# A hybrid conv, state-space and FFN kernel: layer norm variance on all channel partitions, and the conv loop written out

## The reference

```python
x = x + _L0_conv_ref(_gn(x), ...)                 # x is [8, 32, 16, 16]
t = _to_tokens(x)
t = t + _L1_attn_ref(_ln_t(t), ...)               # a selective state-space scan
t = t + _L1_ffn_ref(_ln_t(t), ...)                # a few attention/FFN steps chosen by the data
x = _from_tokens(t, x)

def _ln_t(v, eps=1e-05):
    m = jnp.mean(v, axis=-1, keepdims=True)
    s = jnp.var(v, axis=-1, keepdims=True)
    return (v - m) / jnp.sqrt(s + eps)

# in _L0_conv_ref: nine taps, each sampled bilinearly at learned positions
sampled = bilinear_sample(x, ys, xs)
out = jnp.einsum('bkhwc,ock->bohw', sampled, w)
```

## Time and profile before

| | |
|---|---|
| median of 3 runs | 377.03 us (374.76 to 381.24) |
| the profiled execution | 376.58 us, of which 374.8 us are the span of its instructions |
| PE busy in the span | 268.1 us (72%) |
| DVE busy | 299.2 us (80%) |
| ACT busy | 162.6 us (43%) |
| POOL busy | 238.8 us (64%) |
| mean granted PE clock | 0.750 of full speed |

### The profile page before, as it was taken

The page is one execution under the profiler, slowest core; times in us unless marked ns, Lnnn a source line. Parts: engine busy times, 40 slices in busy tenths (PEclk is TensorE's granted clock), DMA queues, the critical chain, the costliest instruction groups (busy, mean ns, idle before and its releaser), DMA issues. The chain is left out here.

```text
span 374.8 us, 4192 instructions
## 1 busy us (share of the span) xinstructions
PE 268.1 (72%) x1390; PEld 101.5 (27%) x1396; DVE 299.2 (80%) x232; ACT 162.6 (43%) x259; POOL 238.8 (64%) x116
## 2 busy tenths in 40 slices
PE   5987999997862765576547755775567688789883
PEld 1436776664420000000000000000000143236521
DVE  1089999972688999999999999999999974324732
ACT  1064776662535543444434452554354341224420
POOL 1245899980029999999999999999999730000000
PEclk9898999999986555555565556556555599998998
DMA  6000000000020000000000000000000000000000
GB/s 219 33 0 2 2 0 0 0 0 1 23 62 2 0 1 0 0 0 2 0 0 0 0 1 0 2 1 0 0 0 0 1 2 1 12 16 0 0 0 28
DMA packets 2495, 3.83 MB, mean 10 GB/s; under 512 B 687, under 2 KB 1712, under 8 KB 2480
## 3 DMA queue, kind: packets, MB, share of 16 engines
q1 hardware_dynamic: 2348, 3.58, 3.3%
q10 hardware_dynamic: 132, 0.07, 0.1%
HBM read 2.59 MB, written 0.26 MB: 8 GB/s over the span
## 5 line engine op out<-in xcount | busy, mean ns | idle before, releaser
L362 POOL TENSOR_TENSOR pool<-pool 128x1024 f32<-128x1024 f32 x62 | 144.6, 2352 | 37.7 <-DVE pool L645 37.7
L645 DVE TENSOR_TENSOR_SCAN pool<-ps,pool 128x1024 f32<-128x1024 f32 x63 | 143.8, 2283 | 2.0 <-ACT ps L468 2.0
L957 PE MATMUL ps<-pool,picks 96*128 96x512 bf16 x120 | 59.5, 597 | 72.5 <-DVE pool L645 72.5
L466 ACT ACTIVATE ps<-ps,ssmw 128x1020 f32<-128x1020 f32 x64 | 69.4, 1084 | 74.7 <-DVE pool L634 74.7
L963 PE MATMUL ps<-pool,chosen 128*32 128x512 f32 x256 | 60.0, 1033 | 0.7 <-DVE pool L662 0.7
L634 DVE TENSOR_TENSOR pool<-pool,ps 128x1024 f32<-128x1024 f32 x49 | 58.5, 1195 | 1.2 <-PE ps L938 1.2
L957 PEld LDWEIGHTS ps<-pool,picks 96*128 96x128 bf16 x120 | 7.8, 109 | 146.5 <-DVE pool L645 146.5
L418 ACT ACTIVATE pool<-ps 128x1024 f32<-128x1024 f32 x36 | 34.7, 1024 | 20.4 <-PE ps L860 20.4
L860 PE MATMUL ps<-cst,pool 128*128 128x128 f32 x288 | 36.4, 282 | 3.7 <-DVE pool L224 3.7
L356 POOL TENSOR_TENSOR pool<-pool 128x1024 f32<-128x1024 f32 x15 | 35.2, 2346 | 1.5 <-ACT pool L454 1.5
L860 PEld LDWEIGHTS ps<-cst,pool 128*128 128x128 f32 x288 | 32.8, 144 | 10.3 <-issue 10.3
(11 more groups left out here) (128 smaller groups left out, 207.5 us busy)
## 6 DMA issues: line engine op xcount, KB each, us to landing
ssmw<-ssm_w_dram SPq DMA_DIRECT2D x1, 896.0 KB, 8.5
pool<-pool SPq DMA_DIRECT2D x12, 64.0 KB, 2.0
offw<-offset_w_dram SPq DMA_DIRECT2D x1, 576.0 KB, 6.3
cst<-const_dram SPq DMA_DIRECT2D x1, 426.0 KB, 6.8
xq<-x_dram SPq DMA_DIRECT2D x2, 128.0 KB
out_dram<-fin SPq DMA_DIRECT2D x2, 128.0 KB
convw<-conv_w_dram SPq DMA_DIRECT2D x1, 144.0 KB, 6.8
pool<-w_up_dram SPq DMA_DIRECT2D x2, 64.5 KB
```

The costliest lines, as they stand in the source:

```text
L362: pool_e.tensor_tensor(to, of, cn, ALU.mult).then_inc(prod_ready, 1)
L466: act.activation(decay[:, :, 1:HW], decay[:, :, 1:HW], ACT.Exp, scale=wt["a"][:, PER * g + j:PER * g + j + 1]).then_inc(da_ready, 1)
L645: dve.tensor_tensor_scan(state[e % GROUPS], slot(e), dbx[e % GROUPS], 0.0, ALU.mult, ALU.add)\
L957: ins = pe.matmul(slot(e)[:, column_half(c)], picks[:, j * 128:(j + 1) * 128], stack[0:96, g * SEQ + c * BANK:g * SEQ + (c + 1) * BANK], s ...
```

## The change

The conv loop is written out in Python on all four engines, so every index is a constant; PE reads the weights directly from `zs`, and the tile `zk`, its 18 copies on POOL and their semaphore are gone. The turn of the next chunk now also stands ahead of the tap sum at what was the end of a row, and the hats beyond the last chunk are not made. The layer norm sums the squares with one matmul whose weights are `mean` (1/32 in each 32x32 block, made once on POOL), so that the variance stands on all 128 channel partitions and 512 columns; root and reciprocal are taken on that 128x512 tile. The transposes, the widening copy and the second `keep_warm(4)` are gone.

```diff
+        root = sb("root", [128, TOK])
+        mean = sb("mean", [128, 128])
...
-            eng.wait_ge(samp_turned, 6 * it + 2 * j + 2)
+            if it:
+
+                eng.wait_ge(samp_turned, 6 * (it - 1) + 2 * j + 2)
...
+            pool_e.tensor_tensor(mean[:, :], ident, part["centre"], ALU.subtract).then_inc(mean_ready, 1)
...
-            with pool_e.Fori(0, ROWS) as kk:
-                for half in range(HALVES):
-                    it = HALVES * kk + half
-                    sampling_chunk(pool_e, it, 2)
-                    pool_e.wait_ge(z_ready, 8)
-                    for j in range(3):
-                        k = 3 * kk + j
-
-                        pool_e.wait_ge(chunk_summed, 3 * it + j + 1)
-                        pool_e.tensor_copy(zk[j], zs[:, half, :, :, bass.ds(k * C, C)]).then_inc(zk_ready, 1)
-
+            for it in range(HALVES * ROWS):
+                sampling_chunk(pool_e, it, 2)
...
-                act.activation(root[:, :], bank(2)[:, 0:16], ACT.Sqrt, bias=eps[:, :]).then_inc(ln_sd, 1)
+                act.activation(root[:, :], bank(2), ACT.Sqrt, bias=eps[:, :]).then_inc(ln_sd, 1)
...
-            with dve.Fori(0, ROWS) as kk:
-                for half in range(HALVES):
-                    for j in range(2):
-                        sampling_chunk(dve, HALVES * kk + half, j)
-
-                    distances(half, kk + 1)
+            for it in range(HALVES * ROWS):
+                for j in range(2):
+                    sampling_chunk(dve, it, j)
+                if it + HALVES < HALVES * ROWS:
+                    distances(it + HALVES)
...
-                step(dve.reciprocal(inv[:, :], root[:, :]))
+                step(dve.reciprocal(root[:, :], root[:, :]))
                 settle()
-                dve.tensor_copy(inv_wide[:, :].rearrange("p (k c) -> p k c", k=16),
-                                inv[:, :].unsqueeze(2).broadcast_to([128, 16, C])).then_inc(ln_inv, 1)
-                dve.wait_ge(ln_turned, n + 1)
-                return dve.tensor_tensor(dst[:, :], cen[:, :], bank(2), ALU.mult)
+                return dve.tensor_tensor(dst[:, :], cen[:, :], root[:, :], ALU.mult)
...
-            def tap_sum(it, half, j):
-                pe.wait_ge(zk_ready, 3 * it + j + 1)
-                pe.wait_ge(turned_ready, 6 * it + 2 * j + 2 + 3)
+            def tap_sum(it, j):
+                kk, half = divmod(it, HALVES)
+                k = 3 * kk + j
+                pe.wait_ge(turned_ready, 6 * it + 2 * j + 2)
                 for hh in range(2):
                     for q in range(PAIRS):
-                        ins = pe.matmul(bank(0)[quad(q), half * HW:(half + 1) * HW], zk[j][:, q, hh, :],
+                        ins = pe.matmul(bank(0)[quad(q), half * HW:(half + 1) * HW],
+                                        zs[:, half, q, hh, k * C:(k + 1) * C],
                                         sampT[j][:, q, hh, :], start=False, stop=False)
...
-                for c in range(4):
-                    ins = pe.matmul(bank(2)[:, PAIRS * c:PAIRS * (c + 1)], sq[:, c * 128:(c + 1) * 128], part["pairs"],
-                                    start=True, stop=True)
-                ins.then_inc(ln_var, 1)
-                keep_warm(4)
-                pe.wait_ge(ln_inv, n + 1)
-                for c in range(4):
-                    ins = pe.transpose(bank(2)[:, c * 128:(c + 1) * 128], inv_wide[:, c * 128:(c + 1) * 128], ident)
-                ins.then_inc(ln_turned, 1)
+                pe.wait_ge(mean_ready, 1)
+
+                pe.matmul(bank(2), mean[:, :], sq[:, :], start=True, stop=True).then_inc(ln_var, 1)
```

More of the change, by code:

```diff
@@ L76, in hybrid_kernel @@
         sq = sb("sq", [128, TOK])
-        root = sb("root", [128, 16])
-        inv = sb("inv", [128, 16])
-        inv_wide = sb("inv_wide", [128, TOK])
+        root = sb("root", [128, TOK])
+        mean = sb("mean", [128, 128])
         tn = sb("tn", [128, TOK])
@@ L110, in hybrid_kernel @@
         sampT = [region("conv", 8 * HW).rearrange("p (q h n) -> p q h n", q=PAIRS, h=2) for _ in range(3)]
-        zk = [region("conv", 8 * C).rearrange("p (q h o) -> p q h o", q=PAIRS, h=2) for _ in range(3)]
         xs = region("ssm", SEQ)
@@ L181, in hybrid_kernel @@
         samp_made = [sem(f"samp_made{j}") for j in range(3)]
-        samp_turned, turned_ready, zk_ready, chunk_summed, conv_done = map(
-            sem, ["samp_turned", "turned_ready", "zk_ready", "chunk_summed", "conv_done"])
+        samp_turned, turned_ready, chunk_summed, conv_done = map(
+            sem, ["samp_turned", "turned_ready", "chunk_summed", "conv_done"])
         ln_in, ln_cen, ln_sq, ln_var, ln_sd, ln_out = map(
             sem, ["ln_in", "ln_cen", "ln_sq", "ln_var", "ln_sd", "ln_out"])
-        ln_inv, ln_turned = sem("ln_inv"), sem("ln_turned")
+        mean_ready = sem("mean_ready")
         delta_done, xs_done, b_done, gate_in_done, c_done = map(
@@ L220, in sampling_chunk @@
             eng.wait_ge(hat_ready, it + 1)
-            eng.wait_ge(samp_turned, 6 * it + 2 * j + 2)
-            now = hat[:, bass.ds(it, 1), :, 2 * j:2 * j + 2, :].rearrange("p i c o y -> p (i c) o y")
+            if it:
+                eng.wait_ge(samp_turned, 6 * (it - 1) + 2 * j + 2)
+            now = hat[:, it, :, 2 * j:2 * j + 2, :]
             eng.tensor_tensor(samp[j].rearrange("p c (y x) -> p c y x", y=SIDE),
@@ L310, in _ @@
             pool_e.memset(wbd[:, :, :], 0.0).then_inc(wbd_zeroed, 1)
-            pool_e.sem_inc(chunk_summed, 3)
             pool_e.wait_ge(spread_in, 16)
@@ L384, in _ @@
             act.activation(gsd[:, :], mv[:, :, 1], ACT.Sqrt, bias=eps[:, :]).then_inc(gn_sd, 1)
-            act.sem_inc(turned_ready, 3)
             def evacuate_filters(n):
@@ L398, in hats @@
                 act.wait_ge(hat_abs, i + 1)
-                v = hat[:, bass.ds(i, 1), :, :, :].rearrange("p i c o y -> p (i c o y)")
+                v = hat[:, i, :, :, :].rearrange("p c o y -> p (c o y)")
                 act.activation(v, v, ACT.Relu, bias=1.0, scale=-1.0).then_inc(hat_ready, 1)
@@ L407, in _ @@
             evacuate_filters(3)
-            with act.Fori(0, ROWS) as kk:
-                for half in range(HALVES):
[L411 to L422, removed]
+            for it in range(HALVES * ROWS):
+                for j in range(3):
+                    if it:
+                        act.wait_ge(chunk_summed, 3 * (it - 1) + j + 1)
+                    for side in range(2):
+                        s = 2 * j + side
+                        act.wait_ge(samp_turned, 6 * it + s + 1)
+                        act.activation(sampT[j][:, 2 * side:2 * side + 2].rearrange("p q h n -> p (q h n)"),
+                                       bank(2 + 2 * (s % 3), 2), ACT.Copy).then_inc(turned_ready, 1)
+                    if j == 1 and it + HALVES < HALVES * ROWS:
+                        hats(it + HALVES)
             def layer_norm(n):
@@ L558, in _, with distances @@
                .then_inc(off_ready, 1)
[L560 to L563, removed]
+            def distances(i):
+                kk, half = divmod(i, HALVES)
+                pos = bank(1)[:, half * HW:(half + 1) * HW].rearrange("p (c o) -> p c o", c=8)[:, :, 6 * kk:6 * kk + 6]
+                v = hat[:, i, :, :, :]
                 dve.tensor_tensor(v, pos.unsqueeze(3).broadcast_to([128, 8, 6, SIDE]),
@@ L572, in _ @@
             for half in range(HALVES):
-                distances(half, 0)
-            with dve.Fori(0, ROWS) as kk:
-                for half in range(HALVES):
-                    for j in range(2):
-                        sampling_chunk(dve, HALVES * kk + half, j)
-                    distances(half, kk + 1)
+                distances(half)
+            for it in range(HALVES * ROWS):
+                for j in range(2):
+                    sampling_chunk(dve, it, j)
+                if it + HALVES < HALVES * ROWS:
+                    distances(it + HALVES)
             dve.wait_ge(conv_done, 1)
@@ L824, in keep_warm @@
                     pe.matmul(bank(at), zero_bf[:, 0:128], zero_bf[:, :], start=True, stop=True)
-            pe.sem_inc(samp_turned, 6)
             pe.wait_ge(zero_set, 1)
@@ L853, in turn @@
                     s = 2 * j + side
-                    pe.wait_ge(turned_ready, 6 * it + s + 1)
+                    if 6 * it + s >= 3:
+                        pe.wait_ge(turned_ready, 6 * it + s - 2)
                     for q in range(2):
@@ L862, in turn @@
                     ins.then_inc(samp_turned, 1)
-            def tap_sum(it, half, j):
-                pe.wait_ge(zk_ready, 3 * it + j + 1)
-                pe.wait_ge(turned_ready, 6 * it + 2 * j + 2 + 3)
+            def tap_sum(it, j):
+                kk, half = divmod(it, HALVES)
+                k = 3 * kk + j
+                pe.wait_ge(turned_ready, 6 * it + 2 * j + 2)
                 for hh in range(2):
                     for q in range(PAIRS):
```

(9 more changed lines are left out.)

## The result

| | before | after | ratio, 95% interval |
|---|---|---|---|
| first comparison | 375.89 us (4 runs) | 385.95 us (382.51 to 388.74, 4 runs) | 1.024 [1.015, 1.033] |
| second (e7_again below) | 378.72 us (17 runs) | 384.41 us (383.54 to 388.66, 6 runs) | 1.018 [1.011, 1.025] |

By these ratios the changed kernel is slower by about 2%, 7 to 9 us, where +4 us was forecast; the medians lie 10.1 and 5.7 us apart. The ratios leave out runs more than 1.5% above the fastest of the same kernel, the medians don't, and the profiled execution (388.74 us, span 386.9 us) is such a run; where that matters, a second profile of the same kernel stands beside it (e7_again, span 381.8 us). The first median lies 0.95 us above the top of the stated range (385 us), the second within it.

The account below looks back on a forecast made before the run. PE was taken to set the conv loop's pace, held up by copies, and the norms to be pure chains. -2.9 + 2.3 + 1.7 + 2.3 + 0.65 = +4.05 on 376.6 gave 380.65, or 381.0 us in the runs' terms; range 376.5 to 385.

Parts of the forecast that it names:

- The conv loop, -2.9 us: Conv loop: without POOL's copies PE runs 2.90 us a tap to the last, ending 2.9 us sooner.
- the rival of the ports: Conv loop: DVE and POOL contend, PE waits for products, 2.3 us lost, sum 383.3 us; chance 0.12.
- The layer norms, +2.3 us each: Both layer norms: the 128x512 reciprocal at 3.33 us makes each norm 2.3 us longer.
- The line through 128x2 and 128x16: Layer norms: reciprocal's 165 and 252 ns, 6.2 ns an element, extended to 512 elements as 3.33 us.
- PE's clock behind the first norm, +1.7 us: First projections: after PE's 4.9 us pause the clock is 0.50 for 3.4 us, costing L911 1.7 us.
- The rival that the clock stays down: First projections: both groups double, 7.4 us in place of 1.7, sum 386.7 us; chance 0.11.
- PE's clock behind the second norm, +0.65 us: Ahead of L1011: the same pause loses 1.7 us, of which 0.65 shows.
- the 1.06 us to spare: Behind the second norm: PE's slack before L1097, which waits for a weight DMA, taken as 1.06 us.

Follow-up runs that it names:

- e7_again: The changed kernel run once more, unchanged: 384.41 us (6 runs).
- e5_copies: Conv loop written out, layer norms of before, but POOL's 18 weight copies and PE's waits for them put back: 377.89 us, ratio 1.007 to the kernel before.
- e1_conv: The changed kernel with the layer norms of before, so only the conv loop is written out: 373.89 us, ratio 0.995 to the kernel before.
- e3_warm: The changed kernel with 21 matmuls on zeros filling PE's pause in both layer norms: 384.11 us, ratio 1.018 to the kernel before.
- e2_norm: The kernel before with only the new layer norms put in, conv loop of before: 383.27 us, ratio 1.014 to the kernel before.
- e10_bridge: The changed kernel with 3 matmuls on zeros between projections L889 and L882, the norms' pause left: 380.29 us, ratio 1.013 to the kernel before.
- e8_warm_again: The kernel of e3_warm run again, unchanged: 383.37 us (7 runs), ratio 1.013 to the kernel before.
- e9_fill8: The changed kernel with 8 matmuls on zeros, not 21, in PE's pause in each norm: 385.87 us, ratio 1.028 to the kernel before.
- e4_rsqrt: The changed kernel with ACT's Abs_reciprocal_sqrt in place of root and reciprocal, its table brought in ahead: 372.01 us, ratio 0.986 to the kernel before.

## Why the prediction fell short

By its own steps, against the profiles of the changed kernel:

- **The conv loop, -2.9 us.** Measured -2.7 (57.1 to 54.4 us), every tap 2.90 us as forecast; e5_copies shows that the copies carry it, e1_conv that it stands alone. Right in mechanism and size. The hand-written order of DVE and POOL held: the rival of the ports didn't come.
- **The layer norms, +2.3 us each.** Measured +2.4 each. The line through 128x2 and 128x16 gave 3.33 us for the reciprocal; it takes 3.35 in both norms, though the base was fourteen elements. The missing 0.1 us is the root, 0.69 us where the square's 0.60 was taken. The Trainium skill's repeat count of 8 (VectorE: DVE Perf Modes, section on the fixed hardware budget), read as 8 cycles an element, gave an estimate of 4.3 us. The measurement decides: from 252 ns at 16 elements to 3353 ns at 512 it is 6.25 ns an element, six cycles at its 0.96 GHz.
- **PE's clock behind the first norm, +1.7 us.** The clock fell as forecast, but the size of this term was wrong, and it is the step that was off: "the granted clock is 0.50 for 3.4 us" was carried over from the two restarts of the earlier trace rows. Here it was 0.50 for 10.2 us, 9 of them after the restart. L889 lost the 1.7 us, and L882 another 2.1 in full, 3.8 together. e3_warm takes all of it back by filling the pause, and e2_norm shows it without the conv change. The rival that the clock stays down was right in its mechanism, and at 7.4 us for the two groups its price was twice the measured 3.8. The length of a fall wasn't the constant that it was taken for: ahead of the loop, where nothing was changed, the first restart of the earlier trace rows has 3.4 us at 0.50 in the profile of before and 6.8 in both of the changed kernel. Whether the 1.11 us pause behind L889 lengthened it is open; e10_bridge speaks for it, in one profile whose other fall was shorter too.
- **PE's clock behind the second norm, +0.65 us.** Measured +0.46 (11.84 to 12.30 us), and right in its mechanism: the slower matmuls on zeros used up the 1.06 us to spare and 0.45 more. Other profiles with the same pause have 0 to 1.0 us.
- **Not in the sum.** The steps above make -2.7 + 2.4 + 3.8 + 2.4 + 0.5 = +6.4 us, 1.7%, which is within both measured intervals. By its ratio the first comparison shows 9.0 us; the further 2.6 us fit the attention stage, which in the first profile of the changed kernel lost 4.4 us to a fall of the clock against the profile of before, in e7_again gained 0.5, and differs as much between e3_warm and e8_warm_again, which are one kernel. In the spans, 6.4 + 4.4 + 1.5 (the start) = 12.3 us of the 12.1 between the profiles of before and after. The start of the kernel varies too (30.6, 32.1 and 31.5 us to the first turn, the clock at 0.50 for 3.6 or 6.8 us of it). Which fall the attention stage gets goes with the moment at which it begins. In all three profiles with 10.2 us (the changed kernel, e3_warm, e9_fill8) it begins 10.5 to 10.7 us into the stage, in all five with 3.4 us (before, e1_conv, e4_rsqrt, e5_copies, e10_bridge) 5.8 to 6.0 us into it, and four have none. What sets that moment, and why some kernels meet the long fall more often (most of the executions of e3_warm and e8_warm_again, by their times, fewer of before's), is open.

## What to carry to other kernels

Before an operation is moved onto a wider tile, price it by the element from two sizes of the same operation in the trace: here a line through 2 and 16 elements gave the time of 512 to 1%, and an operation that costs six cycles an element is not a small step any more. A pause that a longer step opens on PE is to be priced by what PE does next, as a range: the falls behind such pauses lasted 3.4, 6.8 or 10.2 us here, and the length of one wasn't that of another. Filling the whole pause took the loss back, filling 1.9 of its 5.0 us did not; filling the next short pause too may help, but isn't shown. Copies on POOL beside DVE work with two SBUF inputs cost what they wait for, not what they move: the last one, with DVE idle, took 0.40 us, the median one 2.45.

## What the runs showed of the hardware beyond the expected

- After the pause of 5 us the clock came back only within L882, 9 us after PE had restarted, in four profiles (the changed kernel, e7_again, e2_norm, and e9_fill8 with 3.25 us of pause); in e10_bridge it was back 4.9 us after. The first restart of the earlier trace rows had 3.4 us at 0.50 in five profiles and 6.8 in seven, with the same code there.
- In the attention stage the clock falls to 0.50 without a pause like those of the norms. Before the kernel's change PE was busy for all of the 5.8 us ahead of the fall and all of the 3.4 us in it; in the changed kernel it was busy 9.12 of the 10.40 us ahead, with a pause of 1.11 us, and 10.20 of 10.20 in it. The fall lasts 0, 3.4 or 10.2 us in different executions, and attention to the end then takes 39.1, 39.6 to 39.8 or 44.0 us.
- `Abs_reciprocal_sqrt` on ACT takes 0.69 us on 128x512 from PSUM, as much as `Sqrt`, and does the work of a 3.35 us reciprocal on DVE besides.
